# Moving the head and the router of a three-part language block: heads and late weights into the last layers, top two and gates pair by pair into attention turns and the expert stage

## The reference, cut to what matters

```
# part 1: tokens -> h0
x = emb[tok];  x = x + fast_memory(x);  x = ln(x)
for i in range(4):                       # "layers", 128 -> 512 -> 128
    x = x + gelu(ln_i(x) @ W1[i] + b1[i]) @ W2[i] + b2[i]
h0 = x @ head_W + head_b                 # "head", 128 -> 64
# part 2: linear attention, 4 heads of 32
z  = layernorm(h0)
q, k, v = rmsnorm(z) @ w_qkv             # k and v get 4 memory columns
h1 = h0 + z + rmsnorm((softmax_n(k) v^T) softmax_d(q) @ w_out + b_out)
# part 3: mixture of experts, 8 experts, top 2
xn = ln(layernorm(h1)) * gamma + beta
logits = xn @ Wr + br;  top 2;  w = softmax(top values), spread over 8 experts
out = h1 + sum_e w[e] * (gelu(xn @ W1e + b1e) @ W2e + b2e)
```

## Time and profile before

| | us |
|---|---|
| median of 3 runs | 488.81 |
| the profiled execution's own time | 490.28 |
| its span | 488.5 |
| TensorE busy | 422.5 (86%) |
| VectorE busy | 364.9 (75%) |
| ScalarE busy | 328.7 (67%) |
| GpSimd busy | 281.6 (58%) |

### The profile page before, as it was taken

How to read it: one execution, slowest core, us unless ns; L and a number is a source line. 1 busy time by engine, 2 the same in 40 slices (tenths; PEclk the granted TensorE clock), 3 DMA queues, 4 the chain that set the end, 5 groups by cost and what they waited for, 6 DMA issues and landing times.

```text
span 488.5 us, 6268 instructions
## 1 busy us (share of the span) xinstructions
PE 422.5 (86%) x1965; PEld 339.6 (70%) x1965; DVE 364.9 (75%) x925; ACT 328.7 (67%) x530; POOL 281.6 (58%) x416
## 2 busy tenths in 40 slices
PE   3876499999999999999999676859594899999995
PEld 2664387888888888888779665748482667777773
DVE  4956668999889999999866957787946755666652
ACT  1133478888888888888973345353544588999883
POOL 0234837777777777777304743645644057667673
PEclk9995889999999999999996759596766599999997
DMA  6600011222222212212100000000000000000000
GB/s 238 238 2 0 1 24 23 46 46 49 45 47 52 43 47 43 45 43 45 43 0 2 0 1 1 1 1 1 1 0 1 1 1 12 11 11 12 11 12 21
DMA packets 15832, 14.93 MB, mean 31 GB/s; under 512 B 9780, under 2 KB 10552, under 8 KB 15544
## 3 DMA queue, kind: packets, MB, share of 16 engines
q1 hardware_dynamic: 15800, 14.54, 11.9%
HBM read 13.42 MB, written 1.11 MB: 30 GB/s over the span
## 4 chain that ended last, share of the span: by engine, by line
PE 40%; DVE 30%; ACT 23%; issue 3%; POOL 2%; DMA 1%; SPq 0%; POOLq 0%; DVEq 0%; ACTq 0%
PE ps L1222 34%; DVE hid_lo L867 7%; ACT hid L561 7%; ACT hid_hi L566 6%; DVE xn L857 6%; DVE stats L789 5%; ACT xn_hi L557 3%; PE ps L1420 2%; PE ps L1243 1%; DVE hh L1041 1%; PE ps L1533 1%; ACT x L599 1%; DVE x L813 1%; DVE st L1028 1%; PE ps L1383 1%
## 5 line engine op out<-in xcount | busy, mean ns | idle before, releaser
L867 DVE TENSOR_TENSOR hid_lo<-hid,hid_hi 128x1024 fp32r<-128x1024 f32 x64 | 78.2, 1222 | 23.1 <-ACT hid_hi L566 23.0
L561 ACT ACTIVATE hid<-ps,b_fold 128x512 f32<-128x512 f32 x128 | 83.9, 682 | 15.9 <-PE ps L1222 15.8
L1222 PE MATMUL ps<-xn_hi,w_all 128*128 128x512 f32 x256 | 89.2, 410 | 0.9 <-DVE xn_lo L862 0.9
L1222 PE MATMUL ps<-hid_hi,w_all 128*128 128x512 f32 x256 | 84.2, 390 | 0.0
L566 ACT ACTIVATE hid_hi<-hid 128x1024 fp32r<-128x1024 f32 x64 | 67.9, 1061 | 2.0
L1197 DVE TENSOR_TENSOR hid<-hid,ps 128x512 f32<-128x512 f32 x64 | 43.8, 686 | 33.3 <-ACT hid L709 31.6
L1222 PEld LDWEIGHTS ps<-xn_hi,w_all 128*128 128x128 f32 x256 | 48.8, 190 | 12.7 <-DVE xn_lo L862 2.2
L1222 PEld LDWEIGHTS ps<-hid_hi,w_all 128*128 128x128 f32 x256 | 48.0, 188 | 10.3 <-DVE hid_lo L867 0.4
L1222 PE MATMUL ps<-xn_lo,w_all 128*128 128x512 f32 x128 | 50.5, 395 | 0.0
L1222 PE MATMUL ps<-hid_lo,w_all 128*128 128x512 f32 x128 | 49.9, 390 | 0.0
L709 ACT ACTIVATE hid<-ps,eb_fold 128x512 f32<-128x512 f32 x64 | 43.7, 687 | 8.1 <-PE ps L1222 7.5
(11 more groups left out here) (221 smaller groups left out, 906.3 us busy)
## 6 DMA issues: line engine op xcount, KB each, us to landing
rstd_row<-roots SPq DMA_DIRECT2D x29, 256.0 KB, 4.0
hh<-in_tokens SPq DMA_DIRECT2D x8, 256.0 KB, 7.8
hid<-in_w SPq DMA_DIRECT2D x2, 1024.0 KB, 8.7
out<-hh SPq DMA_DIRECT2D x8, 128.0 KB, 1.9
ew_raw<-in_expert_w SPq DMA_DIRECT2D x1, 512.0 KB, 9.8
roots<-rstd SPq DMA_DIRECT2D x29, 2.0 KB, 1.4
ew_raw<-in_expert_w SPq DMA_DIRECT2D x1, 256.0 KB, 9.9
cons<-in_constants SPq DMA_DIRECT2D x1, 233.0 KB, 2.7
```

What stands on the lines that cost most here:

```text
L561: act.activation(hid[:, j % 2, f, :], bank[f], ACT.Gelu, bias=b1_fold[:, j // B * F + f:j // B * F + f + 1]).then_inc(gelu_done, 1)
L867: dve.tensor_tensor(hid_lo[:, j % 2, 2 * p:2 * p + 2, :], hid[:, j % 2, 2 * p:2 * p + 2, :], hid_hi[:, j % 2, 2 * p:2 * p + 2, :].bitcast( ...
L1222: return pe.matmul(out, lhsT, rhs, start=start, stop=stop)
```

## The change

1. **Heads.** `head(0)` to `head(4)` are issued after `up(27)` to `up(31)`; `head(5)` to `head(7)` between the first `qkv`s. The ring has 2 banks (7, 6). `head_out` and `head_moments` of rows 0 to 3 stand in VectorE's steps 28 to 31. On TensorE `z_transposes(0, 0)` now stands in front of `down(31)`.
2. **Late weights.** The bias folds go to the set-up (after n = 5, bank 5). ScalarE's scaling and rounding go to steps 6, 8, 10, 12 and 14 of the layers, VectorE's parts to steps 10, 14 and 16. The padding memset goes into GpSimd's list of inverse roots, before row 29's.
3. **Router by pairs.** `top_two` is cut into `logits_in`, `first_of_two`, `second_of_two`, `second_one_hot`; `weights` into `weights` and `gates_out`; all work on two rows (64 elements a partition). Pair 0 is done in turn 2, pair 1 in turn 3, pairs 2 and 3 at fixed units n of the expert stage. `scaled_output`, `moments`, `expert_z`, `expert_z_lo` of the last pair are also at units 2, 3, 6, 8.
4. **Banks.** `hidden` has a ring of 2 banks (0, 4) instead of 4; the gate products go to banks 2 and 3; `zst1` keeps two rows instead of eight; `y_sb` lies elsewhere in `scratch`.
5. The gelu table is loaded after `gate(0)` at the end of turn 2's list on ScalarE, instead of before rows 4 and 5 of the router.

```diff
 # GpSimd
             for n in range(B, B * (L + 1)):
                 inverse_root_of_row(n, n % 4)
+                if n == B + 2 * B + 4:
+                    pool.wait_ge(mm2_done, 2 * B)
+                    pool.memset(w_pad[:, :, 4 * E:P], 0.0).then_inc(pad_zeroed, 1)
...
                 if n % E in LO_BY_POOL:
                     hidden_lo(n)
+                if n == 3:
+                    for k in range(2):
+                        expert_norm(B - 2 + k, k)
 # ScalarE
             for j in range(L * B):
+                if j == 6:
+                    late_scales()      # wqkv_g 128x384, wr_g 128x8
+                if j == 8:
+                    expert_scale()     # ew1_raw 128x1024
+                if j == 10:
+                    second_layer_hi()  # ew2 128x512, eb2_hi
+                if j == 12:
+                    projections_hi()   # wqkv, wr
+                if j == 14:
+                    first_layer_hi()   # ew1 128x1024
                 for f in range(F):
                     gelu_of(j, f)
...
+            pair(expert_z_turned, 0)
+            pair(logits_out, 0)
+            act_pair((z_hi,), 6)
+            act_pair((q_turned, attended), 4)
+            act_pair((ez_hi,), 2)
+            act_pair((z_turned, exp_k, k_turned, exp_q, copy_v), 6)
+            gate(0)
+            act.preload_act_table(ACT.Gelu)
+            pair(expert_z_turned, 2)
+            pair(copy_gates, 0)
+            pair(logits_out, 2)
+            act_pair((q_turned,), 6)
+            act_pair((ez_hi,), 4)
+            gate(1)
+            act_pair((attended,), 6)
+            pair(expert_z_turned, 4)
+            pair(copy_gates, 2)
...
+            for n in range(UNITS + 4):   # gelu(n), hidden_hi(n - 1), and
+                # 2, 3: logits_out(4), (5)   7: ez_hi(6), (7)   12: gate(2)
+                # 13, 14: expert_z_turned(6), (7)   17, 18: copy_gates(4), (5)
+                # 21, 22: logits_out(6), (7)   30: gate(3)   34, 35: copy_gates(6), (7)
 # VectorE, layers
                 if j >= 2:
                     residual(j - 2)
+                if j >= L * B - 4:
+                    head_out(j - (L * B - 4))
                 h_lo(j, 0)
+                if j >= L * B - 4:
+                    head_moments(j - (L * B - 4))
                 if 0 < j < L * B - 1:
                     x_lo(j + 1)
                 h_lo(j, 1)
+                if j == 10:
+                    eb2_zeroed = late_smalls()
+                if j == 14:
+                    qkv_lo()
+                if j == 16:
+                    expert_lo(eb2_zeroed)
+            for k in range(2):
+                z_of(k, k)
             residual(L * B - 2)
+            head_out(4)
+            for k in range(2):
+                z_lo(k, k)
+            head_moments(4)
             residual(L * B - 1)
 # VectorE, in dve_turn(2): logits_in(0) after z_lo; first_of_two(0) before max_k;
 # second_of_two(0) before the moments of h1; second_one_hot(0), weights(0), gates_out(0) at the end.
 # turn 3, written out:
+            both(expert_z, 4)
+            both(masked_context, 6)
+            for k in range(2):
+                scaled_m(6 + k, k, v_total)
+            logits_in(1)
+            v = first_of_two(1)
+            both(expert_z_lo, 4)
+            v = second_of_two(1, v)
+            v = second_one_hot(1, v)
+            v = weights(1, v)
+            gates_out(1, v)
+            moments(6, o_ready, ...)
 # VectorE, expert stage, after dve_job(n):
+                # 2: scaled_output(6, 7)   3: moments of h1   6: expert_z   7: logits_in(2)
+                # 8: expert_z_lo   9, 10, 11, 13, 14: top two and gates of pair 2
+                # 24: logits_in(3)   25, 26, 27, 31, 32: top two and gates of pair 3
 # TensorE
                 up(j)
+                if j >= L * B - EARLY_HEADS:
+                    head(j - (L * B - EARLY_HEADS))
                 if j:
                     down(j - 1)
...
+            z_transposes(0, 0)
+            down(L * B - 1)
+            z_transposes(1, 1)
+            head(5)
+            qkv(0, 0)
+            head(6)
+            head(7)
+            pe.wait_ge(h0_ready, B)
+            qkv(1, 1)
+            pair(k_transposes, 0)
...
+            for k in range(2):
+                pe.wait_ge(kt_ready, 4 + k + 1)
+                expert_z_transposes(k)
+            pair(context, 4)
+            pe.wait_ge(late_weights, 1)
+            for b in (0, 1):
+                route(b)
+            for b in (0, 1):
+                logits(b)
+            for step in (q_transposes, projected_context, attend):
+                pair(step, 4)
+            next_rows(6)
+            for k in range(2):
+                pe.wait_ge(kt_ready, 6 + k + 1)
+                expert_z_transposes(2 + k)
+            pair(context, 6)
+            for b in (0, 1):
+                turn_gates(b)
+            for b in (2, 3):
+                route(b)
+            pe.wait_ge(gates_copied, 2)
+            for b in (2, 3):
+                logits(b)
+            for step in (q_transposes, projected_context):
+                pair(step, 6)
+            for b in (4, 5):
+                expert_z_transposes(b)
+            pair(attend, 6)
+            for b in (2, 3):
+                turn_gates(b)
 # TensorE, expert stage, at the end of unit n:
+                # 2: route(4), (5)   5: logits(4), (5)   12: expert_z_transposes(6), (7)
+                # 16: turn_gates(4), (5)   20: route(6), (7)   23: logits(6), (7)   33: turn_gates(6), (7)
```

More of the change, by code:

```diff
@@ L1152, in top_two, with second_of_two @@
                 chain(dve.reduce_max(top[:, 1, r], e1, AX.X))
-                chain(dve.tensor_tensor(o1, e1, each(top[:, 1, r]), ALU.is_equal))
+                own.inc(dve.tensor_tensor(o1, e1, each(top[:, 1, r]), ALU.is_equal))
+                return own.n
+            def second_of_two(p, v):
+                r = rows_of(p)
+                l, o1, e2 = (a[:, r, :] for a in (lg, oh1, eq2))
+                later = back8.unsqueeze(1).broadcast_to([P, GP, E])
+                own.wait(v)
                 chain(dve.scalar_tensor_tensor(l, o1, -3e38, l, ALU.mult, ALU.add))
@@ L1212, in _ @@
                     dve_job(n)
+                if n == 2:
+                    both(scaled_output, 6)
+                if n == 3:
+                    moments(6, h1_ready, lambda b, k: h1[:, b, :], st1, mv1, mv1_ready)
+                if n == 6:
+                    dve.wait_ge(ezlo_ready, B - 2)
+                    both(expert_z, 6)
+                if n == 8:
+                    both(expert_z_lo, 6)
+                if n == 7:
+                    logits_in(2)
+                if n == 9:
+                    v = first_of_two(2)
+                if n == 10:
+                    v = second_of_two(2, v)
+                if n == 11:
+                    v = second_one_hot(2, v)
+                if n == 13:
+                    v = weights(2, v)
+                if n == 14:
+                    gates_out(2, v)
+                if n == 24:
+                    logits_in(3)
+                if n == 25:
+                    v = first_of_two(3)
+                if n == 26:
+                    v = second_of_two(3, v)
+                if n == 27:
+                    v = second_one_hot(3, v)
+                if n == 31:
+                    v = weights(3, v)
+                if n == 32:
+                    gates_out(3, v)
                 if 1 <= n <= UNITS and (n - 1) % E in LO_BY_DVE:
@@ L1341, in down, with head @@
                 last.then_inc(mm2_done, 1)
+            def head(b):
+                pe.wait_ge(x_ready, B * L + b + 1)
+                if b >= 2:
+                    pe.wait_ge(h0_ready, b - 1)
+                for t in range(NT):
+                    last = mm(bank[HEAD_BANK[b % 2]][:, t * D2:(t + 1) * D2], x[:, b, t * P:(t + 1) * P], headw[:, :])
+                last.then_inc(head_done, 1)
             for j in range(L * B):
```

519 lines of the change are left out of this document (258 added, 261 removed).

## The result

The changed kernel took 494.28 us (median of 4 runs, 492.69 to 495.98) against 488.81 for the kernel before (4 runs, 487.84 to 490.13): ratio 1.0111, 95% interval 1.0064 to 1.0158. Forecast were 485.7 and a gain. Timed again beside the experiments it gave 493.44 against 488.41, ratio 1.0082 (1.0050 to 1.0114); from here on, medians leave out runs over 1.5% above the fastest of their kernel, here 6 of 12, five of them at 495.6 to 496.8 and one at 544.37 with a granted clock of 0.72 (with them the median is 495.12). It is slower by about 1%.

The account below looks back on a forecast made before the run. Layers bound by a VectorE-ScalarE ring, with TensorE's row about as long; expert stage seemingly by TensorE. Terms 9.0 - 8.3 + 5.0 - 18.8 + 10.0 = -3.1 gave 487.2, on the median's scale 485.7; range 479 to 494.

Parts of the forecast that it names:

- part 5: Expert stage after `dve_job(5)`: inserted work on TensorE, VectorE, GpSimd and ScalarE adds 10.0 us (bounds +5 and +18).
- The credit that I gave: Expert stage: each VectorE insertion costs its length less 0.87, from 0.52 free per unit and 0.35 allowed lateness; sum 5.8.
- Less 2.5: Expert stage: 2.5 us taken off because stalls meet one another and TensorE's waits for GpSimd's low parts vanish.
- Part 1: Layers, up to `up(31)`: four heads, late weights and the padding memset add 9.0 us.
- Part 2: From `up(31)` to the first Exp: 8.3 us gained (bounds -6 and -10.5), with a new wait before `down(31)`.
- Turns 0 and 1: First two attention turns: periods unchanged, 0 us.
- part 3: Turn 2: router work of rows 0 and 1 makes `context(6)` come 5.0 us late.
- Part 4: From `context(6)` to `dve_job(5)`: 18.8 us gained, bounds -15.3 (clock stays down) and -21.7 (never falls).
- Rival B: Expert stage pays full price, VectorE steps costing their length less 0.52: 18 us there, 493.7 in all; chance 0.22.
- Rival A: TensorE's clock stays up in turns 2 and 3, halving `context`: 5.4 us more gained, 480.3; chance 0.18.
- Rival C: TensorE's clock stays at 1.2 GHz from turn 3 into the expert stage: 489.2; chance 0.15.

Follow-up runs that it names:

- h1_layers: Layers, heads and late weights of the changed kernel, with the rest of the kernel before: 488.88 us, ratio to before 1.0005.
- pool_halves: The changed kernel with GpSimd's subtraction of units 5 to 15 and 22 to 35 done in two halves of 256 elements: 492.44 us.
- no_steps: The changed kernel without 32 of VectorE's router steps (third and fourth pair) in the expert stage: 486.48 us, ratio to before 0.9942.

## Why the prediction was wrong

The step that failed is part 5, "each insertion costs its length less 0.87", "+10.0": the mechanism (insertions into the ring of gelu, job and low part) was right, its size was not. Each VectorE insertion was priced at an undisturbed length. In the trace of the changed kernel 7 router steps stand still for 5.9 us together (L1222, L1231, L1233, L1235, L1253, L1255 and a cast: 1.15, 0.71, 1.12, 1.34, 1.29, 1.19, 0.65 for 0.22, 0.22, 0.17, 0.22, 0.17, 0.22, 0.29), `expert_z` for 2.0 and `expert_z_lo` for 1.1: 9.0 in part 5. The credit that I gave was also too large. The maxima in the kernel before show that even two steps of 0.22, which fit into the 0.52 that a unit has free, cost 0.04 each, where my rule gives nothing. "Less 2.5" for stalls that meet one another was a guess; the trace shows a wait of 2.1 for the gates that came on top. And TensorE's clock has no term in the part: the 16.5 are 8.2 in which TensorE is busy longer (92.3 for 84.1; 5.05 were forecast) and 8.3 in which it is idle longer, and for 8.0 us between 384.7 and 403.0 it runs at the lower clock, where the stage before had 1.00. How the 16.5 divide among these causes is known only in part: not standing still in row 0 gave 3.1 with nothing left out, 6.4 with the fill, and the router's steps with one operand in PSUM 2.6.

That such instructions hold each other up was to be seen in the trace of the kernel before. In the layers, where VectorE's `h_lo` reads two SBUF tensors, GpSimd's product of 4 elements takes 1.16 on average; the same shape on L408, beside an instruction that leaves it alone, 0.20. Groups by line, and the timeline of one such meeting, in the kernel before:

```profile
L411 POOL TENSOR_TENSOR var_in<-var_in 128x4 f32<-128x4 f32 x32 | 37.2, 1163 | 2.6
L408 POOL TENSOR_TENSOR var_in<-stats 128x4 f32<-128x4 f32 x32 | 6.4, 200 | 0.0
```
```profile
102.35 1.22 DVE L867 TENSOR_TENSOR hid_lo<-hid,hid_hi 128x1024 fp32r<-128x1024 f32 x1
102.37 1.26 POOL L411 TENSOR_TENSOR var_in<-var_in 128x4 f32<-128x4 f32 x1
```

The other steps:
- Part 1 (+9.0, came +8.2): right in the sum, partly by luck. VectorE's blocks lie in the ring at full length: the starts of `norm_x` (L904) are 5.97 apart, but 6.57, 6.44 and 8.66 where `late_smalls`, `qkv_lo` and `expert_lo` stand, 3.8 more as forecast. ScalarE's two large blocks lengthen their rows by 0.1, not by 1.0, although `expert_scale` stands in the chain with 1.04 at 110.76. The two rows after `expert_lo` are 1.3 longer for a forecast 1.0, with the memset at 175.5 and TensorE's clock at 0.57 from 174 to 178, not separated.
- Part 2 (-8.3, came -9.5): right, with its wait: `down(31)` took 4.34 for 12 products. Parts 1 and 2 together are -1.3 in the traces (+0.7 forecast), and h1_layers confirms that nothing is gained or lost (0.1).
- Turns 0 and 1 (0, came -1.0) and part 3 (+5.0, came +4.1): right in size.
- Part 4 (-18.8, came -16.0): `scaled_output` at job 2, 3.71 for 1.65, is 2.1 of the 2.8 missing. It is the same fault as in part 5.
- Rival B (493.7, 0.22) names the place and comes nearest to the time, but not the mechanism: it has each step at its undisturbed length less 0.52, with nothing overlapping, and its decision point, part 5 above 13.1, was passed at 16.5.
- Rival A (clock up in turns 2 and 3, 0.18) did not come. In the stretch of the earlier trace rows TensorE was busier, 8.75 of 9 in place of 7.95, and the granted clock was 0.50 as before; turn 3 was at 0.51 again, though its `context` took 4.48 in place of 5.50:

```profile
329.00:338.00 9.00, 8.75 (x37) 6.74 (x36) 4.00 (x16) 2.92 (x7) 5.24 (x8) 0.50 0.00 0
355.00:362.00 7.00, 6.61 (x28) 4.92 (x26) 6.93 (x22) 3.98 (x7) 5.69 (x9) 0.51 0.00 0
```
- Rival C (clock down from turn 3 into the stage, 0.15) came in part: the clock was low in stretches and not throughout, with 0.50 again at 382.5 and 399.6 within the stage, and it differs between executions (last section). Its price was put into part 4 alone.

## What to carry to other kernels

Before a step is moved beside other work, look at what the other engines read there: a small VectorE instruction with two SBUF tensors beside a busy GpSimd lasts as long as the rest of GpSimd's instruction, and one with an operand in PSUM, or a maximum, does not. In a trace look for groups whose mean is far above the shortest of the same shape: that is where a price list taken from quiet stretches fails. Work for a ring that is full on one engine goes in pieces of one or two steps, and its consumer stands two units behind, not one (1.5 us of the stage here, in one execution). After a stall that leaves TensorE idle, look at its clock too: it was at half for 10.2 us of this stage.

## What the runs showed of the hardware that was not expected

Standing still goes both ways: GpSimd's subtraction of 1.28 us took 1.83 in the changed kernel at 425.77, where one of VectorE's (0.68) had started at the same time.

```profile
425.77 0.68 DVE L1309 TENSOR_TENSOR xn_hi<-hid,w_all 128x512 fp32r<-128x512 f32 x1
425.77 1.83 POOL L502 TENSOR_TENSOR xn_hi<-hid,w_all 128x512 fp32r<-128x512 f32 x1 [1.29 <-ACT w_all L747]
```

The granted clock between `context(6)` and gelu(0) differs between executions of the same instructions. Three profiled executions of kernels with one and the same order there: the changed kernel, pool_halves, no_steps (columns as above):

```profile
354.02:374.87 20.85, 17.31 (x86) 14.72 (x86) 15.65 (x72) 9.95 (x20) 7.22 (x14) 0.67 0.00 0
```
```profile
352.10:370.00 17.90, 14.44 (x86) 11.84 (x86) 15.15 (x72) 9.91 (x21) 7.45 (x14) 0.81 0.00 0
```
```profile
352.80:375.37 22.57, 19.31 (x86) 16.63 (x86) 15.65 (x72) 9.95 (x20) 7.20 (x13) 0.55 0.00 0
```

86 instructions of TensorE take 17.9, 20.9 or 22.6 us, at a clock of 0.81, 0.67 or 0.55 on average, with VectorE as busy in each. That is 4.7 us, 1% of the kernel, and a likely source of the wide runs (487.9 to 496.8 for the changed kernel, 486.5 to 491.4 for before, but for one run each of 544.4 and 511.0); the low stretches within the stage, 10.2 us in the changed kernel, 6.8 in no_steps and 3.4 in pool_halves, are another. Either could explain why the medians differ by 5.5 and the two traces by 2.3, which was not shown; what decides it in an execution stays open.
